# A fused linear-attention and feed-forward layer on one core: values of two steps taken together, all masks on VectorE, a third bank for scores

## What is computed

```python
x = x + attn(layernorm(x))
x = x + ffn(layernorm(x))          # ffn has a layernorm of its own (gamma, beta), and adds 0.5*z to its input

# attn: q = elu(proj)+1, k = elu(proj)+1, v = proj; chunks of 128 tokens, state S, z carried on
scores = jnp.where(mask, einsum('bqd,bkd->bqk', qi, ki), 0)      # causal inside the chunk
num = einsum('bqk,bkd->bqd', scores, vi) + einsum('bqd,bde->bqe', qi, S)
den = sum(qi * (cumsum(ki) + z)); out = num / den; then out @ Wo.T + bo

# ffn: w = (q - 128) * scales per group of 128 rows; 1024 hidden features
y = silu(hf @ w1 + fc1_bias); z = y @ w2 + fc2_bias
```

## Time and profile before

| | |
|---|---|
| median of 3 runs | 1586.78 us (1585.32 to 1587.36) |
| profiled execution, its own time | 1583.21 us |
| span of its trace | 1581.5 us |
| granted TensorE clock, mean | 0.991 of full speed |
| TensorE busy | 1538.9 us (97%) |
| VectorE / ScalarE / GpSimd busy | 1230.4 / 1180.0 / 825.7 us |

### The profile page before, as it was taken

How to read it: one execution, slowest core, us unless ns; L and a number is a source line. 1 busy time by engine, 2 the same in 40 slices (tenths; PEclk the granted TensorE clock), 3 DMA queues, 4 the chain that set the end, 5 groups by cost and what they waited for, 6 DMA issues and landing times.

```text
span 1581.5 us, 41041 instructions
## 1 busy us (share of the span) xinstructions
PE 1538.9 (97%) x14820; PEld 1314.4 (83%) x14820; DVE 1230.4 (78%) x2459; ACT 1180.0 (75%) x2045; POOL 825.7 (52%) x594
## 2 busy tenths in 40 slices
PE   5799999999999999999999999999999999999997
PEld 4578888888888888888888888888888888888886
DVE  6678787878787878787878787878787878787865
ACT  3497777797777797777797777797777787777763
POOL 3255445555445555445555445555445555446553
PEclk9899999999999999999999999999999999999998
DMA  7756765546764546664557665556664446764540
GB/s 182 176 129 148 172 156 130 130 124 151 172 159 122 126 131 152 172 170 113 123 130 154 172 150 131 124 129 157 172 161 117 127 126 159 172 160 114 118 102 28
DMA packets 153944, 222.96 MB, mean 141 GB/s; under 512 B 20032, under 2 KB 71488, under 8 KB 153920
## 3 DMA queue, kind: packets, MB, share of 16 engines
q1 hardware_dynamic: 152560, 222.63, 57.4%
q10 hardware_dynamic: 1360, 0.01, 0.0%
HBM read 138.69 MB, written 83.89 MB: 141 GB/s over the span
## 4 chain that ended last, share of the span: by engine, by line
PE 89%; DVE 4%; ACT 2%; issue 2%; DMA 2%; SPq 1%; POOL 0%; DVEq 0%; ACTq 0%
PE ring L322 34%; PE num L489 8%; PE ring L384 8%; PE sc L447 7%; PE ring L385 7%; PE sc L322 5%; PE num L456 4%; PE state_acc L322 3%; PE num L322 3%; DVE probs L607 3%; PE ring L521 2%; PE state_acc L470 2%; ACT silu_f L851 1%; PE num L504 1%; PE num L384 1%
## 5 line engine op out<-in xcount | busy, mean ns | idle before, releaser
L999 POOL TENSOR_TENSOR s_lo<-silu_f,s_hi 128x512 fp32r<-128x512 f32 x256 | 341.0, 1338 | 346.8 <-ACT s_hi L862 346.8
L693 DVE SCALAR_TENSOR_TENSOR silu_f<-ring,scale,silu_f 128x512 f32<-128x512 f32 x222 | 166.3, 749 | 165.6 <-ACT silu_f L851 164.0
L322 PE MATMUL ring<-w_hi,s_hi 128*128 128x256 f32 x992 | 281.3, 284 | 0.7 <-issue 0.7
L322 PE MATMUL ring<-w_hi,s_lo 128*128 128x256 f32 x992 | 278.0, 280 | 0.0
L322 PE MATMUL ring<-w_lo,s_hi 128*128 128x256 f32 x992 | 278.0, 280 | 0.0
L607 DVE TENSOR_TENSOR probs<-sc,causal 128x512 f32<-128x512 f32 x384 | 250.6, 680 | 11.3 <-PE sc L447 7.3
L1019 POOL TENSOR_TENSOR qk<-qk,phi_q 128x512 f32<-128x512 f32 x64 | 82.7, 1292 | 265.5 <-DVE qk L660 265.5
L447 PE MATMUL sc<-q_stack,k_stack 96*128 96x256 f32 x1024 | 189.5, 302 | 12.9 <-DVE probs L607 5.5
L322 PEld LDWEIGHTS ring<-w_hi,s_hi 128*128 128x128 f32 x992 | 186.7, 188 | 14.5 <-issue 13.2
L384 PE MATMUL ring<-gt_hi,w_q 128*128 128x512 f32 x441 | 193.2, 438 | 0.0
L1006 POOL TENSOR_TENSOR probs<-probs,causal 128x512 f32<-128x512 f32 x128 | 165.6, 1294 | 46.8 <-ACT probs L944 46.8
(11 more groups left out here) (188 smaller groups left out, 3889.2 us busy)
## 6 DMA issues: line engine op xcount, KB each, us to landing
k_stack<-k_rows SPq DMA_DIRECT2D x192, 256.0 KB, 4.0
q_stack<-q_rows SPq DMA_DIRECT2D x384, 128.0 KB, 6.0
k_rows<-silu_f SPq DMA_DIRECT2D x128, 256.0 KB, 3.7
q_rows<-probs SPq DMA_DIRECT2D x128, 256.0 KB, 4.1
x_in<-in_x SPq DMA_DIRECT2D x32, 512.0 KB, 7.7
xb<-in_x SPq DMA_DIRECT2D x32, 512.0 KB, 7.3
out<-clip SPq DMA_DIRECT2D x64, 256.0 KB, 7.1
silu_f<-in_q SPq DMA_DIRECT2D x2, 512.0 KB, 9.6
```

The lines of the kernel that those rows point to most:

```text
L322: last = e.matmul(target, a, b, start=(n == 0), stop=(n == 3 * len(pairs) - 1))
L693: f_b.done(e.scalar_tensor_tensor(out=slot, in0=ffn_bank(j, 1, A)[:, :], scalar=scale_1[:, 1, j:j + 1], in1=slot, op0=ALU.mult, op1=ALU.add))
L999: sl.done(e.tensor_tensor(s_lo[:, j, :], silu_f[:, j % SLOTS, :], s_hi[:, j, :].bitcast(F32), ALU.subtract))
```

## The change

- All 16 half-masks of a round are made by VectorE. ScalarE's copies and GpSimd's masks of steps 2 to 5 are gone, and so are their events.
- Scores use three banks: `sc0`, `sc1` and, once its snapshots are taken, `state_acc` (table `SCORES`). A use waits for the mask of the use before.
- Steps go in pairs (2,3), (4,5), (6,7): an FFN slice, the first scores, another slice (or the x transposes), the second scores, then both values of the steps u-1 and u and both products with the state. `RING` is dealt out anew for that order.
- VectorE's order follows: both snapshots after `ffn_sum(2)`, `attention(0)` and `ffn_sum(7)` ahead of `xt_lo`.
- The projections wait for each half of `xt_lo` when they come to it.
- Round 0: `weights_2` goes behind the masks, to before the features; it is staged in `x_hat` and no longer in `x1`. Both splits of these weights go behind the features and the layer norm.
- Round 31: `fc2(1)` and VectorE's `final(0)` move behind the output projection. Round 32: orders of `residual` and of one scaling.

```diff
+        SCORES = {(0, 0): 0, (0, 1): 1, (1, 0): 0, (1, 1): 1, (2, 0): 0, (2, 1): 1, (3, 0): 0, (3, 1): 2,
+                  (4, 0): 1, (4, 1): 0, (5, 0): 2, (5, 1): 1, (6, 0): 0, (6, 1): 2, (7, 0): 1, (7, 1): 0}
+        def score_bank(u, r):
+            return (*sc, state_acc)[SCORES[u, r]]
...
-                    if r and u - 1 in POOL_MASKS:
-                        w.need(copied, 0, POOL_MASKS.index(u - 1))
-                    elif u:
-                        need_masked(w, u - 1, r)
+                    before = score_before(u, r)
+                    if before:
+                        w.need(masked[before[1]], 0, before[0])
+                    elif score_bank(u, r) is state_acc:
+                        w.need(snap, 0)
...
-            for u in range(2, U):
-                if u < 7:
-                    fc1(u + 1)
-                if A and u in (2, 4):
+            for u in range(2, U, 2):
+                if u < U - 2:
+                    fc1(2 * (u // 2) + 1)
+                if u == U - 2:
+                    fc1(FT - 1)
+                if A and u < U - 2:
                     spread_reciprocals(u // 2 - 1)
                 if A:
                     scores(u)
+                if u < U - 2:
+                    fc1(2 * (u // 2) + 2)
+                elif N:
+                    x_transposes()
+                if A:
+                    scores(u + 1)
                     values(u - 1)
+                    values(u)
                     from_state(u - 1)
-                if u == 6 and N:
-                    x_transposes()
+                    from_state(u)
...
             fc2(0)
-            fc2(1)
+            if N:
+                fc2(1)
             if A:
                 w.need(at_l)
                 for n in range(2):
                     pe_tokens(e, w, "o", (gt_hi, gt_lo), f"wo{n}", present, wo_pe)
+            if not N:
+                fc2(1)
...
-                for r in range(1 if u in POOL_MASKS else 2):
+                for r in range(2):
                     mask_half(e, w, u, r)
...
-                copy_scores(j - 1)
                 ffn_silu(j - 1)
```

More of the change, by code:

```diff
@@ L230, in build @@
         sc_pe = ev("sc_pe", U)
[L231 to L241, removed]
+        masked = [ev(f"masked{r}", U) for r in range(2)]
         upd_pe, snap = ev("upd_pe", 1), ev("snap", T)
@@ L281, in free_bank @@
             if use == "v0":
-                w.need(snap, -1)
+                w.need(masked[1], -1)
                 return
@@ L333, in pe_projection @@
             last = pe_split3(e, qk_bank("kq".index(n), m)[:, :], [
-                ((w_hi[n][:, t, cols], w_lo[n][:, t, cols]), (xt_hi[:, t, :], xt_lo[:, t, :])) for t in range(T)])
+                ((w_hi[n][:, t, cols], w_lo[n][:, t, cols]), (xt_hi[:, t, :], xt_lo[:, t, :])) for t in range(T)], lambda t: w.need(xt_l, s, t))
             qk_pe.done(last)
@@ L480, in values @@
                 for r in range(2):
-                    need_masked(w, u, r)
+                    w.need(masked[r], 0, u)
                 w.need(v_sb, 0, c)
@@ L687, in ffn_sum @@
                     return
-                if not A and j + 1 < FT:
+                if not A and 0 < j < FT - 1:
                     ffn_scaled(j + 1)
@@ L694, in ffn_sum @@
                                                 in1=slot, op0=ALU.mult, op1=ALU.add))
+                if not A and j == 0:
+                    ffn_scaled(1)
             def mask(u):
@@ L749, in ve_iteration @@
                         in1=gt_hi[:, t, :].bitcast(F32), op0=ALU.mult, op1=ALU.subtract))
+            if Fn and not A:
+                residual()
             if N:
@@ L754, in ve_iteration, with input_lo @@
                 preparation[0]()
+            def input_lo():
+                if N:
+                    for t in range(T):
+                        ve_lo(e, w, ring_bank(f"xt{t}")[:, :], xt_hi, xt_lo, t, xt_h, 1, xt_l)
             if A:
@@ L760, in ve_iteration @@
             ffn_sum(1)
+            if A:
+                mask(1)
             ffn_sum(2)
             if A:
-                mask(1)
                 snapshots(0)
[L765 to L778, removed]
+                snapshots(1)
+                mask(2)
+            ffn_sum(3)
+            ffn_sum(4)
+            if A:
+                mask(3)
+                mask(4)
+            ffn_sum(5)
+            ffn_sum(6)
+            if A:
+                mask(5)
+                mask(6)
+                attention(0)
+            ffn_sum(7)
+            input_lo()
+            if A:
+                mask(7)
             if A:
                 ve_lo(e, w, qk[:, 0, :], gt_hi, gt_lo, 0, at_h, 0, at_l)
-            if preparation[1]:
-                preparation[1]()
+            if preparation[2]:
+                preparation[2]()
             next_features(0)
@@ L830, in ve_iteration @@
                                                   op0=ALU.mult, op1=ALU.mult))
+            if Fn and not N:
+                final(0)
             if Fn:
```

49 lines of the change are left out of this document (26 added, 23 removed).

## The result

The changed kernel takes **1547.29 us** (median of 4 runs, 1546.40 to 1549.93). The kernel before took 1586.11 beside it (4 runs, 1585.32 to 1587.36). The ratio is 0.9761, with a 95% interval from 0.9747 to 0.9775. The forecast was 1548, with a range from 1532 to 1567.

The account below looks back on a forecast made before the run. TensorE, busy for 97%, was taken as the bound. Gains of 31.5 (rounds), 4.9 (round 0), 0.6 (prologue) and 2 (end) sum to 39.0 us: 1583.2 to 1544.2, plus 3.6 to the median, 1548 us; range 1532 to 1567.

Parts of the forecast that it names:

- Steps between kinds of matmul: TensorE, first part of a round: pairing steps means fewer changes between kinds of matmul, saving 0.83 us a round.
- Waits that go: TensorE, ahead of the scores of step 2, around step 6 and in step 7: waits near 0.75 us vanish.
- the path without a new wait: TensorE up to the projections: if nothing new waited, they would start 1.57 us earlier each round.
- The new wait: TensorE at the first projection: held 0.48 us for `xt_lo`, late behind `attention(0)` and sum 7 on VectorE.
- Three hand-offs with no margin: Starts of slice 4, scores 3 and slice 6, just in time; 0.04 us a round taken off for them.
- 1.05 a round: Net gain of a steady round, 1.09 us less 0.04; 31.5 us over rounds 1 to 30.
- Prologue and round 0: Once-only: round 0's features no longer wait behind the second weights, 4.9 us; prologue projection waits for one `xt_lo`, 0.6.
- The end: Once-only: `fc2(1)` behind the output projection lets the second layer norm start earlier, its transposes together; 2 us, 0 to 4.
- values together save nothing: Rival: second values and second product cost as much as alone; 0.62 us lost, 0.47 a round gained, 1565 us; chance 0.12.
- GpSimd shuts VectorE out: Rival: GpSimd operations run through and delay VectorE's `gt_lo` and the key features; 0.7 us a round, 1558 us; chance 0.15.
- VectorE paces the stretch: Rival, masks of step 1 to `xt_lo`: VectorE's returns cost 0.35 us more each, projection later, 1599 us; chance 0.05.

## Why the prediction was right

The time is 0.7 us from the forecast. That it is so close is luck, since two errors of some 3 us cancel: the profiled execution's own time came out at 1547.2 and not 1544.2, but its distance to the median was 0.1 where I added 3.6. By the terms of the sum:

- **Steps between kinds of matmul, 0.83 a round.** Right: 0.86, from the unpaired version. The second values cost 0.44 (1.01 less 0.57), as the nearest row said. The shares of the pairs are 0.22, 0.30 and 0.33 where I had 0.30, 0.30 and 0.23; in the first a lost 0.10 is in it (fourth point).
- **Waits that go, 0.75, and the path without a new wait, 1.57.** Right: 17.58 less 15.98 is 1.60. Scores 2 go into the slice with no wait (0.56 with the step behind the transposes), scores 7 with 0.65. The run with two banks shows that this part hangs on the third bank.
- **The new wait, 0.48 by `xt_lo`.** Right in size, place and queue; moving sum 7 out of it brought the 0.50 back. Two small errors cancel in the size. TensorE starts 0.06 behind the end of `xt_lo` and not 0.16, and its own way from scores 6 to the projection is 3.40 and not 3.51.
- **Three hand-offs with no margin.** One shows: the first half of scores 3 takes 0.34 to the second half in place of 0.24 (740.42 to 740.76). Slices 4 and 6 start on time. I had taken 0.04 off for all three, and 0.10 is lost at the one. The first part is 1.12 shorter even so, where the sum had 1.05.
- **1.05 a round, 31.5 us.** 30.9: the rounds that I read went from 47.56 to 46.46, a little more than forecast, but the mean round before was 47.49. From state sums to state sums the rounds lie between 47.32 and 47.58, and two of them don't give the mean; the state sums of rounds 1 and 31 do.
- **Prologue and round 0, 5.5 us.** 5.0 in these two traces. But this stretch moves by chance: in the ten traces with the new round 0 the state sums of round 1 start between 85.9 and 89.8, the changed kernel's being the earliest, and in the two with the old one at 90.5 and 90.9. By the means of both groups the gain is 3.4. So the term's size is not confirmed, and no run undoes this part alone. What the trace shows agrees with the mechanism. The features start at 57.48 (forecast 59.1, before 66.44), because the weights are scaled at 55.20 already; the low parts lie ahead of the layer norm's last steps as described, and TensorE waits 2.37 us for `x_hat` there.
- **The end, 2 us (0 to 4).** The step that failed in size: 0.3, and even that is within chance (the masks' move alone, whose end is the old one, has 64.0 behind the state sums, the kernel before 66.0). The trace shows the layer norm's transposes coming together, as I said (1515.88 and 1516.31, four each). I had not looked at what stands ahead of them. Round 31 has no x transposes, since no sequence comes next, so TensorE is early at this place. ScalarE's copy of the attention waits 2.08 us for VectorE and stands ahead of its last two activations; so low part 7 comes late, at 1498.98, TensorE waits 1.84 us until 1499.08 (0.69 before) and then runs the second layer's first matmuls at a lower clock. ScalarE and then GpSimd:

```profile
1494.21 0.63 ACT L991 ACTIVATE gt_hi<-qk 128x512 fp32r<-128x512 f32 x1 [2.08 <-DVE qk L743]
1496.10 2.88 POOL L1028 TENSOR_TENSOR s_lo<-silu_f,s_hi 128x512 fp32r<-128x512 f32 x2 [1.09 <-ACT s_hi L900]
```

Of the rivals, "values together save nothing" would have given 1565: the version with the product between the values measured 1566 and costs 0.33 a pair, where the rival had 0.31. So its price was about right and the condition didn't occur. "GpSimd shuts VectorE out" has its mechanism confirmed, at another operation than the one named, and 0.52 a round for its 0.7. That the relief of other engines is worth something was tested and is nothing. That VectorE paces the stretch did not come near: the stretch still has 0.2 us gaps ahead of its masks (748.96), though VectorE is busy for 14.10 of 16.46. No run was made that lengthens its operations.

## What to carry to other kernels

Where one engine is busy for 97%, look inside its busy time: the same matmuls in an order with fewer changes between kinds of matmul took 0.86 us less of a 47.5 us round, and start-to-start distances show it, which the busy share doesn't. Such an order makes results fall due in bunches, so it needs a buffer more (without the third bank 27.5 of 39 us were lost) and a new look at the queues of the engines that serve it: one operation in the wrong place cost 14 us. And look at the first and the last round apart from the steady one: what is placed well in the loop can hold up its end.

## What the runs showed of the hardware

- **The clock after a hole.** In the changed kernel TensorE stands for 0.99 and then 1.84 us in round 31 and has a granted clock of 0.82 in the stretch behind it, with matmuls 0.21 us apart where they take 0.12 (the lower of its two levels, 1.2 GHz, and the upper, 2.4):

```profile
1498.00:1516.00 18.00, 16.92 (x122) 16.95 (x123) 5.15 (x18) 2.80 (x6) 5.41 (x3) 0.82 0.05 17
```

  With the 1.84 closed and the 0.98 still there, the same matmuls ran 0.12 apart. The kernel before waited 0.69 there and kept its clock. The wait alone doesn't tell what follows. With the same two waits 24 matmuls ran 0.21 apart in the changed kernel and 18 in the version with the low part first. All these kernels also wait 1.84 ahead of round 32's first slices: the changed kernel went on there at 1.00 (1518 to 1530), the kernel before at 0.50 (1552.3 to 1559.1). What makes the difference was not tried apart.
- **Both sides can lose at the SBUF ports.** VectorE's `gt_lo` made a GpSimd operation of 2.38 us take 2.83, and a GpSimd operation of 2.41 made a VectorE operation of 0.68 take 2.22. VectorE's operations with one input in PSUM kept their 0.68 to 0.75 beside it.
- **The way back is dear too.** From a 128-row product to the quarter-array values behind it it is 0.42 us, and 0.25 into a slice: 0.17 for the change of form.
